# Layer norm variances by four 32-column products over moving squares, own token kept by a mask

## The chip, the cores and the metric

The kernel runs on one core of one Trainium2 chip. A core has five engines that run side by side and meet only through semaphores: TensorE (matrix products, here PE, its weight loads PEld), VectorE (DVE), ScalarE (ACT), GpSimd (POOL) and SyncE (SP, which issues transfers). The metric is the time of one execution on the device in microseconds; shorter is better.

## The reference

Sixteen layers follow each other on an activation `x` of 4 batches, 512 tokens and 128 features. Each adds to `x` what an attention, an expert or feed-forward stage, a state space stage or a recurrent cell makes of the normalised `x`:

```python
def _layernorm(x, axis=-1, eps=1e-05):
    m = jnp.mean(x, axis=axis, keepdims=True)
    v = jnp.var(x, axis=axis, keepdims=True)
    return (x - m) / jnp.sqrt(v + eps)

x = x + _L0_attn_a_ref(_layernorm(x, axis=-1), ...)
x = x + _L0_ffn_ref(_layernorm(x, axis=-1), ...)
... # fourteen more of the same kind
```

So there are 16 x 4 = 64 norms of one batch, 512 tokens by 128 features each. The change touches only how their variances are found and spread.

## The kernel before

**Layout.** `x` and its normalised copy `xn` stay on chip as 128 partitions (the features) by 4 x 512 columns (the tokens of the four batches). A layer works through the batches one after the other; each engine has its own program, written out by hand as a loop over steps, and waits on semaphores where it needs another's result. All constants and weights are loaded by SyncE at the start (`build_program`, L4198; four groups after layer 2), the constants (`const`) right behind `x`, and the first product waits for both.

**One norm of one batch.** Features lie along partitions, so sums over features are products:
- `centre` (L245): TensorE multiplies by (identity minus 1/128), which leaves x minus its mean in a PSUM bank, 128 x 512.
- `square` (L252): ScalarE squares the bank into on-chip memory; `keep` (L259, or L266 on ScalarE) copies the centred values.
- `var` (L273): for each of the TT = 4 tiles of 128 tokens, a product with the tile's squares as the weights (128 x 128) and one column of 1/128 as the moving side. The result is one column: the variance of token p of tile t stands in partition p, column t of the same bank. A float32 product is two weight loads and two matmuls in the records.
- `eps` (L281): VectorE adds 1e-5 to those 128 x 4 numbers, into `small`.
- `rstd` (L287): GpSimd raises them to the power -1/2.
- `diag` (L294): VectorE multiplies the identity, repeated four times, by them: four diagonal 128 x 128 matrices side by side, 128 x 512.
- `spread` (L302): TensorE multiplies by ones, so that every partition has all tokens' factors, 128 x 512.
- `scale` (L310): VectorE multiplies the kept values by it, into `xn`.

**Where it stands.** `NextNorm` (L192) gives these steps to a layer: while a layer works on a later batch, it normalises the finished ones for the next layer, and its steps are put by hand into the layer's loops. The norm of the last batch (`last=True`, names with `in_`) is mostly done at the start of the next layer. Layer 0 has nothing before it, so `normalise` (L113) does its four norms alone, with the same steps at L136 (centre), L142 (variance), L149 (spread), L156, L164, L168, L173 and L180. The order on each engine is fixed by the program: `eps` and `diag` stand in VectorE's queue between the layer's own operations, `rstd` in GpSimd's.

**Layers by kind.** First attention (lines 317 to 594), expert stages (595 to 984, four of the layers), keep (985 to 1653), linear (1654 to 2067), bit (2068 to 2174, two), landmark (2175 to 2826), pairs (2827 to 3051), cell (3052 to 3221, two), state space (3222 to 3777, two), elu (3778 to 4155). In the expert stages L680, L681 and L701 are the experts' products, L687 a product that spreads gates, L747 and L757 VectorE's steps between them. L1228 (keep), L3867, L3871 and L3855 (elu) and L1882 (linear) are products and a VectorE step of those layers; L3527 is the scan of the state space layers.

Of the kernel before, what the change touches and what calls it, by code (L numbers as in the profile page):

```python
# [15 lines left out]
ALU = mybir.AluOpType  # L16
ACT = mybir.ActivationFunctionType
AX = mybir.AxisListType

B, S, D = 4, 512, 128  # L20
P = 128
TT = S // P
LN_EPS = 1e-5
NEG = -1e30
# [86 lines left out]


def normalise(nc, core, name):  # L113
    L = Layer(nc, name, core, [],
              centred=B,
              square=B,
              kept=B,
              var=B,
              eps=B,
              rstd=B,  # L120
# [3 lines left out]
    with L.ctx:  # L124
        centred, square = L.sb("centred", [P, B, S]), L.sb("square", [P, B, S])
        small = L.sb("small", [P, 2, B, TT])
        diag = L.sb("diag", [P, B, TT, P])
        banks = L.ps("banks", [P, B, S])
        ps_var = L.ps("ps_var", [P, B, S])
        eye = core.w("const", "eye")  # L130
        with nc.Block() as block:
            @block.tensor
            def _(pe):
                for step in range(B + 3):
# [4 lines left out]
                    if 0 <= b < B:  # L139
                        pe.wait_ge(L["square"].sem, L["square"].at(0, b + 1))  # L140
                        for t in range(TT):
                            mm = pe.matmul(ps_var[:, b, t:t + 1], square[:, b, t * P:(t + 1) * P],  # L142
                                           core.w("const", "mean", 0, 1), start=True, stop=True)
                        mm.then_inc(L["var"].sem, 1)
# [14 lines left out]
            def _(dve):  # L159
                for step in range(B + 3):  # L160
# [5 lines left out]
                    if 0 <= b < B:  # L166
                        dve.wait_ge(L["var"].sem, L["var"].at(0, b + 1))
                        dve.tensor_scalar(small[:, 0, b, :], ps_var[:, b, 0:TT], LN_EPS, None, ALU.add)\  # L168
                            .then_inc(L["eps"].sem, 1)
                    b = step - 2  # L170
                    if 0 <= b < B:
                        dve.wait_ge(L["rstd"].sem, L["rstd"].at(0, b + 1))
                        dve.tensor_tensor(diag[:, b, :, :], eye.unsqueeze(1).to_broadcast([P, TT, P]),  # L173
                                          small[:, 1, b, :].unsqueeze(2).to_broadcast([P, TT, P]), ALU.mult)\
                            .then_inc(L["diag"].sem, 1)
                    b = step - 3
# [15 lines left out]
class NextNorm:  # L192


    NAMES = ("centred", "square", "kept", "var", "eps", "rstd", "diag", "spread", "xn")
    SIGNALS = {f"nx_{n}": B for n in NAMES}
    LAST = {f"in_{n}": 1 for n in NAMES}

    def __init__(self, L, *banks, steps=1, last=False, shared=None, buffers=None, elsewhere=None, wide=False):
        self.L, self.banks, self.steps, self.last = L, banks, steps, last  # L200
        key = "in" if last else "nx"
        self.first = B - 1 if last else 0
        self.elsewhere = elsewhere or {}
        self.sets = len(banks) if wide else 1
        if buffers:
            self.kept, self.square_sb, self.diag_sb = buffers
            self.small = L.sb(key + "_small", [P, 2, TT])
        elif shared:
            self.kept, self.square_sb, self.small, self.diag_sb = shared.kept, shared.square_sb, shared.small, shared.diag_sb
        else:  # L210
            self.kept = L.sb(key + "_kept", [P, len(banks), S])
            n = self.sets
            self.squares, self.smalls = L.sb(key + "_square", [P, n, S]), L.sb(key + "_small", [P, n, 2, TT])
            self.diags = L.sb(key + "_diag", [P, n, TT, P])
            self.square_sb, self.small, self.diag_sb = self.squares[:, 0, :], self.smalls[:, 0, :, :], self.diags[:, 0, :, :]
        self.centred, self.squared, self.copied, self.var_in, self.eps_in, self.powered, self.diag_in, self.spread_in, \
            self.xn = (L[f"{key}_{n}"] for n in self.NAMES)

# [49 lines left out]
    def var(self, pe, b):  # L268
# [3 lines left out]
        for t in range(TT):  # L272
            mm = pe.matmul(self.bank(b)[:, t:t + 1], self.square_of(n)[:, t * P:(t + 1) * P],  # L273
                           self.L.core.w("const", "mean", 0, 1), start=True, stop=True, skip_group_check=True)
        mm.then_inc(self.var_in.sem, 1)

    def eps(self, dve, b):
        n = b - self.first
        dve.wait_ge(self.var_in.sem, self.var_in.at(0, n + 1))
        dve.wait_ge(self.powered.sem, self.powered.at(0, self.reused(n)))  # L280
        dve.tensor_scalar(self.small_of(n)[:, 0, :], self.bank(b)[:, 0:TT], LN_EPS, None, ALU.add).then_inc(self.eps_in.sem, 1)  # L281

# [7 lines left out]
    def diag(self, dve, b):  # L290
        n = b - self.first
        dve.wait_ge(self.powered.sem, self.powered.at(0, n + 1))
        dve.wait_ge(self.spread_in.sem, self.spread_in.at(0, self.reused(n)))
        dve.tensor_tensor(self.diag_of(n)[:, :, :], self.L.core.w("const", "eye").unsqueeze(1).to_broadcast([P, TT, P]),  # L294
                          self.small_of(n)[:, 1, :].unsqueeze(2).to_broadcast([P, TT, P]), ALU.mult)\
            .then_inc(self.diag_in.sem, 1)

# [3956 lines left out]
def constants():  # L4254
# [10 lines left out]
        "centre": eye - np.float32(1 / D),  # L4265
        "mean": np.full((P, P), 1 / D, np.float32),
        "eye": eye,
# [165 lines left out]
```

## Time and profile before

| | |
|---|---|
| median of 3 runs | 2679.58 us |
| lowest and highest | 2677.96 and 2688.18 us |
| profiled execution, first to last instruction | 2684.0 us |
| TensorE busy | 2287.6 us, 85% |
| VectorE busy | 1742.8 us, 65% |
| ScalarE busy | 1209.6 us, 45% |
| GpSimd busy | 612.0 us, 23% |
| mean granted clock of TensorE | 0.923 |

The profile is of one execution. Busy time is the union of an engine's instructions; a matmul's record is longer than the time after which the next can start, so start-to-start times say more than durations. The granted clock is a share of 2.4 GHz; the other level is 1.2 GHz. In the views, `128*128` is the part of the array that a product takes (rows by columns), `xN` the number of records, and what stands in brackets is the engine's idle time before the instruction and what ended it.

### The profile page before, as it was taken

To read this page: it belongs to the slowest core of one execution; us is meant where nothing else is said; L and a number is where in the kernel's file an instruction comes from. 1 tells how busy PE (TensorE), PEld (TensorE's weight loads), DVE (VectorE), ACT (ScalarE), POOL (GpSimd) and SP (SyncE) were. 2 spreads that over 40 slices of the span, in tenths; PEclk is the share of its full clock that TensorE was granted. 3 is DMA by queue.
4 is the path that set the end of the run, shared out by engine and by line. 5 is a ranking of instruction groups with operands and counts; after the bars stand their busy time and mean duration, and the time that the engine had idled before them with its cause. 6 is when DMAs were issued, how large, how long until landed. Compare 5 with 4: busy or idle time off the path is not lost. (4 is left out here: it accounts for less than half of the span.)

```text
span 2684.0 us, 29577 instructions
## 1 busy us (share of the span) xinstructions
PE 2287.6 (85%) x9624; PEld 994.5 (37%) x9664; DVE 1742.8 (65%) x2454; ACT 1209.6 (45%) x2392; POOL 612.0 (23%) x606
## 2 busy tenths in 40 slices
PE   8999999957569989887999789977879988978877
PEld 3333334412112224354454334423334436533333
DVE  4666665567877735553463754489995446579995
ACT  3555563157647842221342244265544422256542
POOL 1111110042211110021101010056651023046651
PEclk9999999968879979997867889989999999989999
DMA  3000000032000011000000000022110000012110
GB/s 153 1 1 1 1 1 0 0 48 39 10 2 1 1 43 52 1 1 1 0 1 0 0 1 0 1 80 71 64 39 0 1 0 2 1 64 71 63 55 16
DMA packets 19254, 59.67 MB, mean 22 GB/s; under 512 B 2272, under 2 KB 8480, under 8 KB 18208
## 3 DMA queue, kind: packets, MB, share of 16 engines
q1 hardware_dynamic: 18240, 57.01, 6.8%
q10 hardware_dynamic: 864, 0.79, 0.2%
q8 instruction: 79, 1.29, 0.2%
q14 instruction: 71, 0.58, 0.1%
HBM read 50.12 MB, written 1.31 MB: 19 GB/s over the span
## 5 line engine op out<-in xcount | busy, mean ns | idle before, releaser
L3761 POOL TENSOR_TENSOR l_drive<-l_du,l_bsb 128x1024 f32<-128x1024 f32 x126 | 299.8, 2389 | 142.0 <-DVE l_state L3527 113.0
L3527 DVE TENSOR_TENSOR_SCAN l_state<-l_decay,l_drive 128x1024 f32<-128x1024 f32 x128 | 292.8, 2289 | 13.4 <-ACT l_decay L3468 2.1
L3357 PE MATMUL l_py<-l_read,w_const 128*128 128x512 f32 x512 | 261.6, 636 | 0.0
L287 POOL TENSOR_TENSOR l_nx_small<-l_nx_small,w_const 128x4 f32<-128x4 f32 x50 | 53.7, 1075 | 891.6 <-DVE l_nx_small L281 891.6
L3468 ACT ACTIVATE l_decay<-l_delta,l_a 128x511 f32<-128x511 f32 x256 | 165.7, 681 | 169.1 <-DVE l_state L3527 168.9
L426 ACT ACTIVATE l_probs<-l_psp,l_stats 128x512 f32<-128x512 f32 x256 | 173.1, 683 | 150.4 <-DVE l_stats L436 150.4
L1301 DVE TENSOR_REDUCE l_tops<-l_ring 128x2 f32<-128x1024 f32 x128 | 151.5, 1220 | 45.1 <-PE l_ring L1292 44.7
L434 DVE TENSOR_REDUCE l_stats<-l_psp 128x2 f32<-128x1024 f32 x128 | 156.2, 1221 | 35.6 <-PE l_psp L388 35.0
L742 DVE SCALAR_TENSOR_TENSOR l_product<-l_psu,w_gated,l_first 128x512 f32<-128x512 f32 x104 | 78.1, 751 | 134.5 <-ACT l_first L716 134.2
L1373 ACT ACTIVATE l_shared<-l_ring 128x512 f32<-128x512 f32 x256 | 138.9, 598 | 48.9 <-PE l_ring L1363 48.7
L3537 DVE TENSOR_TENSOR l_read<-l_state,l_pc 128x1024 f32<-128x1024 f32 x128 | 153.3, 1198 | 2.9 <-DVE l_state L3527 1.6
L3341 PE MATMUL l_pc<-l_parts,l_spread 96*128 96x512 bf16 x128 | 52.5, 410 | 107.0 <-DVE l_read L3537 106.9
L716 ACT ACTIVATE l_first<-l_psg,w_gated 128x512 f32<-128x512 f32 x104 | 71.4, 687 | 150.9 <-PE l_psu L681 150.9
L3357 PEld LDWEIGHTS l_py<-l_read,w_const 128*128 128x128 f32 x512 | 105.4, 206 | 90.1 <-issue 85.4
L1187 ACT ACTIVATE l_shared<-l_ring,l_mins 128x512 f32<-128x512 f32 (+3 forms) x256 | 121.1, 541 | 39.0 <-PE l_acc L1228 20.2
L388 PE MATMUL l_psp<-l_q,l_k 64*128 64x512 f32 x512 | 127.6, 616 | 1.1 <-ACT l_probs L426 1.1
L757 DVE TENSOR_TENSOR l_held<-l_held,l_psc 128x512 f32<-128x512 f32 x152 | 103.7, 682 | 37.8 <-PE l_psc L687 30.4
L400 PE MATMUL l_ps_ctx<-l_probs,l_vs 128*64 128x512 f32 x512 | 124.2, 605 | 0.5 <-POOL l_vs L475 0.5
L475 POOL TENSOR_TENSOR l_vs<-l_v,l_stats 128x128 f32<-128x128 f32 x128 | 51.3, 401 | 313.8 <-DVE l_stats L442 313.8
L1172 DVE TENSOR_REDUCE l_mins<-l_ring 128x2 f32<-128x1024 f32 (+2 forms) x96 | 99.4, 1039 | 30.9 <-PE l_ring L1155 29.8
L680 PE MATMUL l_psg<-xn,w_gated 128*128 128x512 f32 x208 | 108.1, 602 | 3.3 <-DVE l_product L742 2.6
L681 PE MATMUL l_psu<-xn,w_gated 128*128 128x512 f32 x208 | 106.4, 593 | 0.0
(608 smaller groups left out, 4330.5 us busy)
## 6 DMA issues: line engine op xcount, KB each, us to landing
l_bsb<-l_rows SPq DMA_DIRECT2D x64, 512.0 KB, 3.6
l_stack<-l_parts SPq DMA_DIRECT2D x84, 64.0 KB
w_gated<-in_gated SPq DMA_DIRECT2D x1, 3297.5 KB, 12.4
w_mha<-in_mha SPq DMA_DIRECT2D x1, 2568.5 KB, 13.2
w_ssm<-in_ssm SPq DMA_DIRECT2D x2, 1171.0 KB, 16.4
w_moe<-in_moe SPq DMA_DIRECT2D x1, 2248.0 KB, 18.1
w_const<-in_const SPq DMA_DIRECT2D x1, 1325.0 KB, 7.5
x<-x_in SPq DMA_DIRECT2D x1, 1024.0 KB, 4.7
```

The lines of the kernel that those rows point to most:

```text
L388: mm = pe.matmul(psp[:, u, i, :], k[r, g % 2, kt * P:(kt + 1) * P], q[r, g % 2, :], start=True, stop=True)
L400: mm = pe.matmul(ps_ctx[i * HD:(i + 1) * HD, :], vs[:, s % 4, i, :], probs[:, s % 4, i, :], start=half == 0 and u == 0, stop=half == 1 and ...
L426: act.activation(probs[:, s % 4, i, :], psp[:, s % 2, i, :], ACT.Exp, bias=stats[:, s % 4, 1, i:i + 1], scale=scale, accum_out=stats[:, s ...
L434: dve.tensor_reduce(stats[:, s % 4, 0, :], psp[:, s % 2, :, :], AX.X, ALU.max).then_inc(L["top"].sem, 1)
L1187: act.activation(probs1[qt][:, g, :], ring[:, at + i, lo:lo + N], ACT.Exp, bias=mins[:, s, n:n + 1], scale=-1.0, **kept).then_inc(L["exp1" ...
L1301: dve.tensor_reduce(tops[:, n % 2, t, :], ring[:, 2 * (x % 2):2 * (x % 2) + 2, :], AX.X, ALU.min)\
L1373: act.activation(probs2[:, p % 3, 2 * (x % 2) + i, :], ring[:, 4 + i, :], ACT.Exp, scale=-1.0)\
L3357: mm = pe.matmul(py[:, t, :], eye, read[:, k % 2, t, :], start=False, stop=k % NS == NS - 1, skip_group_check=True)
L3468: act.activation(decay[:, k % 2, t, 1:], delta[:, b % 2, t, 1:], ACT.Exp, scale=a[:, t, n:n + 1])\
L3527: dve.tensor_tensor_scan(state[:, k % 2, :, :].rearrange("p t s -> p (t s)"), decay[:, k % 2, :, :].rearrange("p t s -> p (t s)"), drive[: ...
L3537: dve.tensor_tensor(read[:, k % 2, :, :], state[:, k % 2, :, :], pc[:, :].unsqueeze(1).to_broadcast([P, CT, S]), ALU.mult).then_inc(L["rea ...
L3761: pool.tensor_tensor(drive[:, k % RING, :, :], du[:, :, :], bsb[:, k // 2 % RING, k % 2, :].unsqueeze(1).to_broadcast([P, CT, S]), ALU.mult)\
```

## The change

The squares become the moving side and the weights a 128 x 32 block of 1/128. For tile t the product goes to array columns 32t to 32t+31 and thereby to partitions 32t to 32t+31 of the bank, 128 columns wide: every one of those 32 partitions has the variance of all 128 tokens of the tile. One token of each four-token set belongs to a partition: partition 32t + m keeps the tokens m, 32 + m, 64 + m and 96 + m of tile t. VectorE adds epsilon and multiplies by a 0/1 mask (`own`, four identities of 32 side by side, in all four quarters) in one operation, 128 x 128, and sums each 32 columns in a second, 128 x 4; it waits for its own first result in between. `small` then has 128 x 4 numbers as before, in another order. `diag` multiplies a constant mask of 128 x 512 (`own_token`) by them, so that again each column has one non-zero entry; power, spread and scale are as they were. The constants lose 96 columns of `mean` and gain 128 of `own` and 512 of `own_token`, 544 more columns of 128 float32. Each norm has one more semaphore.

```diff
@@ normalise @@
                         for t in range(TT):
-                            mm = pe.matmul(ps_var[:, b, t:t + 1], square[:, b, t * P:(t + 1) * P],
-                                           core.w("const", "mean", 0, 1), start=True, stop=True)
+                            mm = pe.matmul(ps_var[t * QUAD:(t + 1) * QUAD, b, 0:P], core.w("const", "mean"),
+                                           square[:, b, t * P:(t + 1) * P], start=True, stop=True,
+                                           tile_position=(0, t * QUAD))
...
-                        dve.tensor_scalar(small[:, 0, b, :], ps_var[:, b, 0:TT], LN_EPS, None, ALU.add)\
+                        dve.scalar_tensor_tensor(own[:, b, :], ps_var[:, b, 0:P], LN_EPS, core.w("const", "own"), ALU.add,
+                                                 ALU.mult).then_inc(L["own"].sem, 1)
+                        dve.wait_ge(L["own"].sem, L["own"].at(0, b + 1))
+                        dve.tensor_reduce(small[:, 0, b, :], own[:, b, :].rearrange("p (j c) -> p j c", j=TT), AX.X, ALU.add)\
                             .then_inc(L["eps"].sem, 1)
...
-                        dve.tensor_tensor(diag[:, b, :, :], eye.unsqueeze(1).to_broadcast([P, TT, P]),
-                                          small[:, 1, b, :].unsqueeze(2).to_broadcast([P, TT, P]), ALU.mult)\
-                            .then_inc(L["diag"].sem, 1)
+                        dve.tensor_tensor(diag[:, b, :, :].rearrange("p t (j c) -> p t j c", j=TT), own_tokens(core),
+                                          by_token(small[:, 1, b, :]), ALU.mult).then_inc(L["diag"].sem, 1)
@@ class NextNorm: var, eps, diag @@
         for t in range(TT):
-            mm = pe.matmul(self.bank(b)[:, t:t + 1], self.square_of(n)[:, t * P:(t + 1) * P],
-                           self.L.core.w("const", "mean", 0, 1), start=True, stop=True, skip_group_check=True)
+            mm = pe.matmul(self.bank(b)[t * QUAD:(t + 1) * QUAD, 0:P], self.L.core.w("const", "mean"),
+                           self.square_of(n)[:, t * P:(t + 1) * P], start=True, stop=True, skip_group_check=True,
+                           tile_position=(0, t * QUAD))
         mm.then_inc(self.var_in.sem, 1)
...
-        dve.tensor_scalar(self.small_of(n)[:, 0, :], self.bank(b)[:, 0:TT], LN_EPS, None, ALU.add).then_inc(self.eps_in.sem, 1)
+        own = self.own[:, n % self.sets, :]
+        dve.scalar_tensor_tensor(own, self.bank(b)[:, 0:P], LN_EPS, self.L.core.w("const", "own"), ALU.add, ALU.mult)\
+            .then_inc(self.own_in.sem, 1)
+        dve.wait_ge(self.own_in.sem, self.own_in.at(0, n + 1))
+        dve.tensor_reduce(self.small_of(n)[:, 0, :], own.rearrange("p (j c) -> p j c", j=TT), AX.X, ALU.add)\
+            .then_inc(self.eps_in.sem, 1)
...
-        dve.tensor_tensor(self.diag_of(n)[:, :, :], self.L.core.w("const", "eye").unsqueeze(1).to_broadcast([P, TT, P]),
-                          self.small_of(n)[:, 1, :].unsqueeze(2).to_broadcast([P, TT, P]), ALU.mult)\
-            .then_inc(self.diag_in.sem, 1)
+        dve.tensor_tensor(self.diag_of(n)[:, :, :].rearrange("p t (j c) -> p t j c", j=TT), own_tokens(self.L.core),
+                          by_token(self.small_of(n)[:, 1, :]), ALU.mult).then_inc(self.diag_in.sem, 1)
@@ constants @@
-        "mean": np.full((P, P), 1 / D, np.float32),
+        "mean": np.full((P, QUAD), 1 / D, np.float32),
+        "own": np.tile(np.eye(QUAD, dtype=np.float32), (TT, TT)),
+        "own_token": np.kron(np.eye(TT, dtype=np.float32), np.tile(np.eye(QUAD, dtype=np.float32), (1, TT))),
```

`QUAD` is 32. `own_tokens` gives the mask as partition by tile t, group j, column c; `by_token` repeats the four numbers over the tiles and over the 32 columns of a group.

## Rows read from the trace of the kernel before

**Rows 1.** The page's first part, and the cores view: span and granted clock.

```profile
PE 2287.6 (85%) x9624; PEld 994.5 (37%) x9664; DVE 1742.8 (65%) x2454; ACT 1209.6 (45%) x2392; POOL 612.0 (23%) x606
...
core 0: 2684.0 us, clock 0.923
```

**Rows 2.** Stretches; busy us (x) of PE, PEld, DVE, ACT, POOL; clock, DMA, GB/s.

```profile
31.20:414.00 382.80, 375.18 (x1316) 121.56 (x1316) 252.35 (x492) 220.78 (x579) 54.19 (x131) 1.00 0.00 1
...
1567.80:1739.10 171.30, 167.30 (x469) 76.64 (x476) 83.40 (x139) 72.79 (x117) 9.12 (x8) 0.99 0.00 1
...
2361.70:2646.90 285.20, 219.51 (x512) 89.69 (x512) 262.50 (x185) 149.50 (x222) 164.29 (x74) 0.93 0.18 60
```

**Rows 3.** Timeline of TensorE in a bit stage: start us, busy us, line, form.

```profile
1262.65 1.02 PE L2092 MATMUL l_out<-l_h,w_bitffn 128*128 128x512 f32 x2
1263.51 0.95 PE L273 MATMUL l_first<-w_const,l_in_square 128*128 128x1 f32 x8
1264.32 1.10 PE L2084 MATMUL l_up<-xn,w_bitffn 128*128 128x512 f32 x2
```

**Rows 4.** Timeline of TensorE in keep: four products of 32 columns.

```profile
596.14 0.43 PE L1228 MATMUL l_acc<-l_shared,l_unit 128*32 128x128 f32 x8
596.50 0.39 PE L1150 MATMUL l_ring<-l_stack 64*128 64x512 bf16 x2
```

**Rows 5.** Timeline of TensorE where the form changes, in keep and in elu.

```profile
610.77 1.12 PE L1063 MATMUL l_aux<-xn,w_keep 128*128 128x512 f32 x2
...
2222.65 0.94 PE L3867 MATMUL l_mix<-l_feats,l_state 128*128 128x128 f32 x6
2223.51 1.08 PE L3871 MATMUL l_mix<-l_energy,l_vaug 128*32 128x128 f32 x32
```

**Rows 6.** Timeline of VectorE: three dependent 128x128 steps of an expert stage.

```profile
1591.26 0.27 DVE L801 TENSOR_REDUCE l_small<-l_tie 128x16 f32<-128x128 f32 x1
1591.57 0.29 DVE L803 TENSOR_TENSOR l_chosen<-l_tie,l_small 128x128 f32<-128x128 f32 x1
1591.90 0.29 DVE L807 SCALAR_TENSOR_TENSOR l_key<-l_chosen,l_key 128x128 f32<-128x128 f32 x1
```

**Rows 7.** The first stretch, all weight loads running; GB/s is last.

```profile
0.00:9.40 9.40, 0.00 (x0) 0.00 (x0) 0.00 (x0) 0.08 (x1) 0.19 (x4) 1.00 0.82 326
```

**Rows 8.** Timeline of TensorE in layer 0's own norm.

```profile
13.06 1.71 PE L142 MATMUL n_ps_var<-w_const,n_square 128*128 128x1 f32 x8
14.63 2.05 PE L136 MATMUL n_banks<-x,w_const 128*128 128x512 f32 x2
16.47 1.71 PE L142 MATMUL n_ps_var<-w_const,n_square 128*128 128x1 f32 x8
```

**Rows 9.** Timeline of the linear stage, VectorE and TensorE.

```profile
1192.85 0.69 DVE L1882 TENSOR_TENSOR l_gated<-l_mix,l_u 128x512 f32<-128x512 f32 x1 [5.70 <-ACT l_square L1819]
1193.46 0.15 DVE L281 TENSOR_SCALAR l_nx_small<-l_last 128x4 f32<-128x4 f32 x1
1193.53 0.68 DVE L1873 TENSOR_TENSOR l_state<-l_front,w_const 128x512 f32<-128x512 f32 x1
...
1195.48 0.70 PE L302 MATMUL l_last<-l_nx_diag,w_const 128*128 128x512 f32 x1 [2.34 <-DVE l_nx_diag L294]
```

**Rows 10.** Timeline of an expert stage behind L281.

```profile
493.95 0.68 DVE L757 TENSOR_TENSOR l_held<-l_held,l_psc 128x512 f32<-128x512 f32 x1
...
494.81 0.19 PEld L701 LDWEIGHTS l_out<-l_held,w_moe 128*128 128x128 f32 x1 [0.24 <-DVE l_held L757]
495.24 1.02 PE L701 MATMUL l_out<-l_held,w_moe 128*128 128x512 f32 x2
```

**Rows 11.** Timeline of the elu stage, VectorE and TensorE.

```profile
2263.03 0.16 DVE L281 TENSOR_SCALAR l_nx_small<-l_last 128x4 f32<-128x4 f32 x1 [1.67 <-PE l_last L273]
...
2265.09 1.13 PE L302 MATMUL l_last<-l_nx_diag,w_const 128*128 128x512 f32 x2 [0.41 <-DVE l_nx_diag L294]
```

**Rows 12.** Timeline of a state space stage: what follows L281 (1971.11, 0.15) on VectorE.

```profile
1971.33 2.29 DVE L3527 TENSOR_TENSOR_SCAN l_state<-l_decay,l_drive 128x1024 f32<-128x1024 f32 x1
```

More of the change, by code:

```diff
@@ L22 @@
 TT = S // P
+QUAD = P // TT
 LN_EPS = 1e-5
@@ L104, in batch, with own_tokens, by_token @@
         return self.x[:, bass.ds(b * S, S)]
+def own_tokens(core):
+    return core.w("const", "own_token").rearrange("p (t j c) -> p t j c", t=TT, j=TT)
+def by_token(rstd):
+    return rstd.unsqueeze(1).unsqueeze(3).to_broadcast([P, TT, TT, QUAD])
 def normalise(nc, core, name):
@@ L118, in normalise @@
               var=B,
+              own=B,
               eps=B,
@@ L126, in normalise @@
         small = L.sb("small", [P, 2, B, TT])
+        own = L.sb("own", [P, B, P])
         diag = L.sb("diag", [P, B, TT, P])
@@ L129, in normalise @@
         ps_var = L.ps("ps_var", [P, B, S])
-        eye = core.w("const", "eye")
         with nc.Block() as block:
@@ L192 @@
 class NextNorm:
-    NAMES = ("centred", "square", "kept", "var", "eps", "rstd", "diag", "spread", "xn")
+    NAMES = ("centred", "square", "kept", "var", "own", "eps", "rstd", "diag", "spread", "xn")
     SIGNALS = {f"nx_{n}": B for n in NAMES}
@@ L206, in __init__ @@
             self.kept, self.square_sb, self.diag_sb = buffers
-            self.small = L.sb(key + "_small", [P, 2, TT])
+            self.small, self.own = L.sb(key + "_small", [P, 2, TT]), L.sb(key + "_own", [P, 1, P])
         elif shared:
             self.kept, self.square_sb, self.small, self.diag_sb = shared.kept, shared.square_sb, shared.small, shared.diag_sb
+            self.own = shared.own
         else:
@@ L214, in __init__ @@
             self.diags = L.sb(key + "_diag", [P, n, TT, P])
+            self.own = L.sb(key + "_own", [P, n, P])
             self.square_sb, self.small, self.diag_sb = self.squares[:, 0, :], self.smalls[:, 0, :, :], self.diags[:, 0, :, :]
-        self.centred, self.squared, self.copied, self.var_in, self.eps_in, self.powered, self.diag_in, self.spread_in, \
+        self.centred, self.squared, self.copied, self.var_in, self.own_in, self.eps_in, self.powered, self.diag_in, self.spread_in, \
             self.xn = (L[f"{key}_{n}"] for n in self.NAMES)
```

## The prediction, made before the changed kernel had run

> **What bounds the kernel now.** I read the page's engine line and the cores view first: one core, 2684.0 us, TensorE busy for 85% of it, mean granted clock 0.923 [rows 1]. Then the stretches view, cut by layer: in the first attention and the expert stages TensorE is busy for 98% and VectorE for 66 and 49%; the two bit stages, not shown, are of that kind with 95%. In the state space stages it is VectorE with 92% [rows 2]. So a norm's work on TensorE counts in one kind of stage and its work on VectorE in the other. In the rest (landmark, linear, pairs, keep, elu) I went to the timeline around each variance step (L273) and asked two things: does the VectorE step behind it (L281) wait for the products or stand in VectorE's queue, and does TensorE wait for the end of the chain (L302)?
>
> **The products, old.** In a bit stage at 2.4 GHz the eight records of L273 (a float32 product is two) run from 1263.51 to the next line's start at 1264.32: 0.81 us for eight one-column outputs, set by eight weight loads at 0.10 apiece. The pair that follows is busy 1.10 us where the pair before was 1.02, so 0.08 of its load shows too: 0.89 us in all [rows 3]. The first load is hidden behind the product before.
>
> **The products, new.** L1228 has the new form exactly: four products of 32 weight columns over 128 float32 columns into four partition quarters of one bank. Its eight records take 0.36 us to the next start [rows 4]. To that come the two ends, where the array goes from 128*128 to 128*32 and back and the load isn't hidden: six records of L3867 last 0.86 us before L3871 starts, where 0.11 each would be 0.66 and one exposed first load 0.10, so some 0.10 goes to the change of form; the pair after L1228 is busy 1.12 us against 1.02, 0.10 more [rows 3, 5]. New block: 0.10 + 0.36 + 0.10 = 0.56 us, a saving of 0.33. Bounds: 0.14 (each change of form costs twice that) to 0.53 (neither costs anything).
> The Trainium skill, page "TensorEngine Tiling (Array Packing)", section "Tiling Modes", speaks against this change: switching the tiling mode, not just the tile, drains TensorE. With a drain of a whole 128-column record at each end the block would be near 0.8 us and the forecast some 6 us later, near 2678; the rows just used show changes of form at 0.10 each, so I go by them.
>
> **The variance step on VectorE.** Removed: one 128x4 operation of 0.15 us that overlaps its successor, starting 0.07 before it [rows 9]. Added: a 128x128 scalar_tensor_tensor, a wait of VectorE for its own result, and a 128x128 reduction. The same shapes: reduction 0.27, scalar_tensor_tensor 0.29, and from the start of the first of such a dependent pair to the start of the next 0.31 to 0.33 us [rows 6]. So 0.33 + 0.20 (the reduction, less the overlap with what follows) in place of 0.07 to 0.08: **0.44 us more** on VectorE's queue and on the chain to GpSimd's power. Bounds 0.40 to 0.60. What is queued behind it on VectorE waits; so does GpSimd's L287. The product with the mask (L294) keeps its 128x512 output; its mask is now read in full instead of repeated, and I take nothing for it (bounds -0.05 to +0.1).
>
> **The sum, norm by norm (64 of them).**
> (1) Constants grow by 544 columns, 272 KB; the load stage moves 326 GB/s, and TensorE's first product waits for it [rows 7]: +0.9 us (0 to 1.5).
> (2) The stand-alone norm of layer 0, four batches. TensorE runs at 1.2 GHz there (L142 takes 1.57 us, the pair L136 1.84, and a batch 3.41) [rows 8]. I double the new block: 1.1 in place of 1.57, four times, less 0.44 for the last chain: -1.4 us. VectorE's own work per batch, three steps of 0.68 and the two new ones, 2.6 us, bounds the gain at about -3.
> (3) TensorE-bound blocks: 3 in the first attention, 16 in the expert stages, 6 in the bit stages, 2 in the landmark stage, 1 in a cell: 28 x 0.33 = -9.2 us. Cover: VectorE's 0.44 lies in its idle time, 34 to 51% of these stages [rows 2]. It shows at six blocks of the expert stages where L757 stands right behind L281: L757 ends at 494.63, the load of L701 starts at 494.81, its product at 495.24, and a load needs 0.11, so the slack is 0.32; 6 x 0.12 = +0.7 [rows 10].
> (4) Chains on which both engines wait in turn and L281 waits for the products, as at 2263.03 (1.67 idle, then TensorE 0.41 at L302) [rows 11]: three such chains follow a product of 32 columns, where no change of form is paid on the way in and the first load isn't exposed twice: I estimate 1.0 us falling to 0.3, less 0.44, so 3 x -0.3. Seven more lie at 1.2 GHz, where the products take 1.57 and more [rows 8] and by the doubled block some 0.9 less with the wait for the load, less 0.44: 7 x -0.5. Together -4.4.
> (5) Chains on which L281 is already late because VectorE is at something else: in the linear stage L1882 is at work from 1192.85, L281 follows at 1193.46, and TensorE then idles 2.34 us for L302 [rows 9]. Faster products gain nothing there and the 0.44 is exposed: 3 in the linear stage, 2 in the pairs, 1 each in keep, landmark, elu: 8 x 0.44 = +3.5.
> (6) State space stages: VectorE goes from L281 straight into the scan [rows 12]; four of the eight norms there have no slack: +1.8.
> Sum: 0.9 - 1.4 - 9.2 + 0.7 - 4.4 + 3.5 + 1.8 = **-8.1 us**. The profiled run's span was 2684.0, so its like would be 2675.9; that run lies 4.4 above the median of 2679.6 and inside the three runs (2678.0 to 2688.2). From the median: **2671.5 us**. A difference below 0.5% (13.4 us) is about what a measurement of this kernel can't tell from none, and this forecast lies inside it.
>
> **The rivals.**
> B, the clock comes back sooner. With a mean of 0.923, 15% of the span, some 410 us, is at 1.2 GHz [rows 1]. The one-column products give the array next to nothing to do: in the start stage TensorE is busy end to end from 9.5 to 28.8 us and its pairs still take 1.84 [rows 8]. The new ones stream 128 columns and are followed sooner by real work. If a tenth of the 410 us went back to 2.4 GHz, with TensorE setting half of it, that is 410 x 0.1 x 0.5 x 0.5 = 10 us more: **2661**. Against: most slow stretches come from waits for scans, maxima and L294, which stay.
> C, the slower side: VectorE's two dependent operations, at their upper bound of 0.60 us and with no slack behind L281 anywhere. Then 64 x 0.60 = 38.4 and 0.9 for the constants stand against the products' 9.2, 1.8 and 8.8 (terms 3, 2 and 4 without VectorE's part): +19.5, **2699**; at 0.44 it would be +9.3, 2689. It decides where the slack behind L281 is under the difference of 0.60 and 0.33. Against: VectorE idles 34 to 51% of the stages in question, and the slack found is 0.32.
> D, the change doesn't do what it says: the four products don't overlap. Then eight passes of 0.107 and the ends make 1.16 us in place of 0.89: 28 x 0.27 = 7.6, and with nothing gained in (2) and (4) 5.6, 0.9, 0.7, 3.5 and 1.8 for the rest: +20, **2700**. Against: L1228's 0.36 for the same form [rows 4].
> E, the 0.33 is given back: TensorE comes sooner to a wait for VectorE or ScalarE and stands there. Without term (3): **2680.5**. For: the first attention has all engines in lockstep. Against: almost no idle is shown before TensorE's products there.
>
> **How the numbers follow.** The forecast has 0.49, with its own range of 2664 to 2677 (the bounds of the block alone give -5.6 and +5.3 on 28 blocks); B 0.24, E 0.13, C 0.09, D 0.05. Faster by over 0.5% (under 2666.2): B's 0.23 and 0.10 of the forecast, 0.33. Slower by over 0.5% (over 2693): 0.06 of C and D's 0.05, 0.11. Within: the rest, 0.56. Leaving out C and D and 6 in 100 at the ends, the range is 2658 to 2684.
>
> **What would show each step.** In the profile after: L273's eight records 0.36 us to the next start, and the 128x128 form on 128*32; the pair behind them at 1.12; the two VectorE steps at 0.29 and 0.27 with 0.03 between; the expert stages 1.1 to 1.4 us shorter each, the bit stages 1.0, the linear stage 1.3 longer, the state space stages 0.9 longer; the first product 0.9 later. The forecast is wrong if the mean clock moves by more than 0.003, if the expert stages don't shorten, or if the products start one after another.

## The result, and the profile after

The changed kernel took 2661.1 us (median of 4 runs, 2659.5 to 2665.8) against 2682.5 for the kernel before on the same chip (4 runs, 2678.0 to 2688.2): a ratio of 0.9933, 95% interval 0.9909 to 0.9956. Measured once more, beside two of the experiments, it gave 2663.3 (6 runs, 2656.6 to 2668.7) against 2681.0, ratio 0.9932 [0.9908, 0.9956]. So it is some 18 us faster by the ratio, 0.67% (21 by the medians): more than the 13.4 us that I had called indistinguishable, though the low end of the interval, 0.44%, isn't. It is inside the range, 10 us below the forecast, and a gain of more than twice the forecast 8.1.

The page and the cores view of the kernel after, to be held against [rows 1]:

```profile
PE 2251.3 (85%) x9624; PEld 933.3 (35%) x9664; DVE 1758.9 (66%) x2518; ACT 1209.4 (45%) x2392; POOL 611.5 (23%) x606
...
core 0: 2664.0 us, clock 0.923
```

TensorE has 36 us less work and 61 us less of weight loads in the same number of instructions, VectorE 16 us more in 64 more. The mean clock is that of before. The span went from 2684.0 to 2664.0, 20.0 less. Where it came from is read stage by stage, each from the first instruction of its lines to the first of the next stage's; "at 1.2" is the time in the stage for which the trace's record of the granted clock shows 1.2 GHz (it has nothing for the start stage):

| stage | before, us (at 1.2) | after, us (at 1.2) | difference | forecast |
|---|---|---|---|---|
| start, with layer 0's own norm | 31.2 | 25.9 | -5.4 | -0.5 |
| first attention | 382.8 (0) | 381.5 (1) | -1.3 | -1.0 |
| four expert stages | 586.8 (11) | 579.5 (7) | -7.4 | -4.6 |
| two bit stages | 84.1 (6) | 81.0 (5) | -3.0 | -2.0 |
| linear | 133.7 (42) | 136.3 (46) | +2.6 | +1.3 |
| landmark | 144.9 (89) | 146.5 (86) | +1.6 | -0.2 |
| pairs | 80.5 (34) | 83.5 (41) | +3.0 | +0.9 |
| keep, elu, two cells | 667.6 (153) | 668.0 (157) | +0.5 | -3.9 |
| two state space stages | 572.2 (79) | 561.7 (68) | -10.5 | +1.8 |

(The seven 1.2 GHz chains of term (4), -3.5, which the forecast didn't place by stage, are all put into the row of keep, elu and the cells.) Seven of the nine rows missed the forecast by more than 1 us, and in opposite directions. The stretches that answer to [rows 2], and the start:

```profile
25.90:407.40 381.50, 373.88 (x1317) 118.95 (x1317) 253.50 (x495) 220.67 (x579) 54.09 (x132) 1.00 0.01 2
1562.60:1730.60 168.00, 163.83 (x469) 72.51 (x475) 85.11 (x144) 72.79 (x117) 9.12 (x8) 1.00 0.00 1
2347.30:2626.70 279.40, 214.64 (x512) 84.55 (x512) 259.29 (x190) 149.44 (x222) 164.35 (x74) 0.95 0.19 61
0.00:25.90 25.90, 11.96 (x49) 3.67 (x49) 9.59 (x20) 3.67 (x5) 5.36 (x8) 1.00 0.93 383
```

In the state space stage VectorE (the third busy figure) has less to do than before, 259.3 against 262.5 us, with five more operations. That is the surprise of this case: something on VectorE got cheaper that the change wasn't about.

The new block on TensorE, in a bit stage, timeline as in [rows 3]:

```profile
1266.42 1.02 PE L2114 MATMUL l_out<-l_h,w_bitffn 128*128 128x512 f32 x2
1267.37 0.43 PE L290 MATMUL l_aux<-l_nx_square,w_const 128*32 128x128 f32 x8
1267.73 1.13 PE L2106 MATMUL l_up<-xn,w_bitffn 128*128 128x512 f32 x2
```

From L290's first start to the next line's 0.36 us, where L273 had 0.81; the pair behind it 1.13, so 0.11 for the change of form on the way out; and on the way in 0.95 from L2114's first start to L290's, 0.09 more than the 0.86 after which L273 began [rows 3]. Together 0.56, as built up from L1228. (By the Trainium skill's "TensorEngine Tiling (Array Packing)", section "Tiling Modes", the array drains at a change of mode; what these rows show of it is 0.1 us each way.)

One caution for all that follows. Stages whose code is untouched differ between executions with the clock. The keep stage of the old form lasted 464.6, 460.1, 458.2 and 457.8 us in four profiles, with 136, 106, 106 and 109 us of it at 1.2 GHz. With the new form it lasted 464.5 us in the changed kernel, and in six further profiles of this study 454.6 to 463.5. The kernel before ran from 2667.0 to 2693.0 in the course of this study. So below I compare stages, and totals only as medians.

### The profile page after: what moved, and what is told of

Same layout as the page of the kernel before. It is cut to its first block and busy times, and to the rows that moved or that the text cites. A ratio compares the mean times of both kernels' runs of the same rounds, so it can differ in the third digit from the quotient of the medians.

```text
span 2664.0 us, 29641 instructions
## 1 busy us (share of the span) xinstructions
PE 2251.3 (85%) x9624; PEld 933.3 (35%) x9664; DVE 1758.9 (66%) x2518; ACT 1209.4 (45%) x2392; POOL 611.5 (23%) x606
## 5 line engine op out<-in xcount | busy, mean ns | idle before, releaser
L3783 POOL TENSOR_TENSOR l_drive<-l_du,l_bsb 128x1024 f32<-128x1024 f32 x126 | 299.8, 2389 | 136.3 <-DVE l_state L3549 108.4
L723 PE MATMUL l_out<-l_held,w_gated 128*128 128x512 f32 x208 | 106.1, 593 | 0.3 <-issue 0.3
```

The costliest lines, as they stand in the source:

```text
L3783: pool.tensor_tensor(drive[:, k % RING, :, :], du[:, :, :], bsb[:, k // 2 % RING, k % 2, :].unsqueeze(1).to_broadcast([P, CT, S]), ALU.mult)\
```

## The experiments

**The start stage: what brought 5.4 us?** Two kernels. The first has the new form in `normalise` alone, the other 60 norms as before (larger constants kept). The second has no new form at all (larger constants kept here too), but in `normalise` the old products stream 128 columns each, and VectorE's 128x4 step reads every 128th column of what they write:

```diff
-  mm = pe.matmul(ps_var[:, b, t:t + 1], square[:, b, t * P:(t + 1) * P],
-                 core.w("const", "mean", 0, 1), start=True, stop=True)
+  mm = pe.matmul(ps_var[:, b, t * P:(t + 1) * P], square[:, b, t * P:(t + 1) * P],
+                 core.w("const", "mean", 0, 1).to_broadcast([P, P]), start=True, stop=True)
```

> The new form in the stand-alone norm of layer 0 alone; the other 60 norms keep the old products, the 128x4 step and the identity as mask. The larger constants stay. My forecast's step (2): the start stage 0.5 us shorter (-1.4, +0.9 for the constants), its pairs still at 1.84 us. Clock theory: the new products give the array columns to stream, so the clock is at 2.4 GHz again from about 14.5 us on, pairs at 1.0 to 1.1 us, start stage 25.9 us in place of 31.2 (-5.4), and the total about 5 below the kernel before. If the rest of the start stage's gain came from somewhere else than the norm, the stage stays above 29.

> All norms old. In the stand-alone norm of layer 0 alone the old products, squares as weights and as many weight loads as before, stream 128 equal columns each instead of one; the variance step then reads every 128th column. No product is shorter, no VectorE operation is added, results are the same. If the clock answers to the columns that go through the array: 2.4 GHz comes back as early as in the new form, the start stage shortens by 3 to 5 us although each block has more to do. If only the shorter block matters (less work at 1.2 GHz, an earlier end of the stage): the stage gets 0 to 2 us longer, at 1.2 GHz to its end.

Measured: new form alone, start stage 25.4 us, every layer but keep and the expert stage before it within 0.2 of before; total 2674.8 us, ratio 0.9994 [0.9979, 1.0010]. Old form with 128 columns, start stage 26.4 us, total 2672.7, ratio 0.9979 [0.9963, 0.9996]. The timeline of TensorE in the second kernel (columns as in [rows 3]), to be held against [rows 8]:

```profile
13.80 1.92 PE L154 MATMUL n_ps_var<-w_const,n_square 128*128 128x128 f32 x8
15.51 1.23 PE L148 MATMUL n_banks<-x,w_const 128*128 128x512 f32 x2
16.58 1.05 PE L154 MATMUL n_ps_var<-w_const,n_square 128*128 128x128 f32 x8
17.47 1.02 PE L148 MATMUL n_banks<-x,w_const 128*128 128x512 f32 x2
```

The first block is longer than the old one (1.71 to the next start, against 1.57), as more columns go through at the 1.2 GHz level. But the pair behind it takes 1.23 and the next 1.02, where the kernel before had 2.05 [rows 8]; there it stayed at that level for all but the last record of the stage:

```profile
24.87 4.82 PE L149 MATMUL n_banks<-n_diag,w_const 128*128 128x512 f32 x6
```

The six records start 0.99, 0.85, 0.85, 0.85 and 0.68 us apart, and the last, at 29.10, is 0.59 us long. The stretches view shows a clock of 1.00 for all of this, and can't be used: the trace's record of the granted clock has no entry before its first one at 2.4 GHz. That entry stands at 28.8 us in the kernel before and at 28.7 and 30.0 in the two other profiles with one-column blocks in this stage; in the ten profiles with 128 columns per product, new form or old, it stands at 13.5 to 15.9. The number of weight loads is the same and VectorE has no added operation. The blocks of the two kernels differ in nothing but the columns that the products stream: with one column each TensorE was busy by the record, and the clock stayed at 1.2 GHz; with 128 each it came up 13 us sooner, though each block had more to do. At 13.5 us, in the first kernel, the rise even came 0.27 us ahead of its first new block, so the first two pairs alone can be enough; in the kernel before they were not, and it did not come between the one-column blocks that followed. It was rival B's mechanism, shown at the one place where it had been sitting in plain view: in [rows 8] TensorE is busy from end to end and slow. The changed kernel has it too:

```profile
14.10 0.53 PE L154 MATMUL n_ps_var<-n_square,w_const 128*32 128x128 f32 x8
14.56 1.12 PE L148 MATMUL n_banks<-x,w_const 128*128 128x512 f32 x2
```

The total of the first kernel moved by less than its start stage (3.1 us by the medians, with an interval that contains both 0 and 5.4), so what the 5.4 is worth in the total is known only to some 3 us.

**The state space stages: what brought 10.5 us?** By-form groups of the product with the mask whose output is `l_square`, before and after (line engine op, out<-in, form, count; then busy us and mean ns):

```profile
L294 DVE TENSOR_TENSOR l_square<-w_const,l_nx_small 128x512 f32<-128x512 f32 x8 | 17.6, 2200 | 2.2 <-POOL l_nx_small L287 2.2
```

```profile
L317 DVE TENSOR_TENSOR l_square<-w_const,l_nx_small 128x512 f32<-128x512 f32 x8 | 9.0, 1125 | 2.2 <-POOL l_nx_small L310 2.2
```

8.6 us of the 10.5 are there, and they come from four of the eight. Two more, the first of each stage, take 2.35 us in both kernels: at 1746.08 before, 0.08 us behind the start of a GpSimd cast (L3743, 1.89 us), and at 1737.49 after, just as far behind the same cast. The change left those as they were. One of the four in the timeline of VectorE and GpSimd, before and after:

```profile
1974.63 2.34 POOL L3761 TENSOR_TENSOR l_drive<-l_du,l_bsb 128x1024 f32<-128x1024 f32 x1
1974.64 2.88 DVE L294 TENSOR_TENSOR l_square<-w_const,l_nx_small 128x512 f32<-128x512 f32 x1
```

```profile
1966.27 0.73 DVE L317 TENSOR_TENSOR l_square<-w_const,l_nx_small 128x512 f32<-128x512 f32 x1
1966.41 2.80 POOL L3783 TENSOR_TENSOR l_drive<-l_du,l_bsb 128x1024 f32<-128x1024 f32 x1
```

Before, GpSimd's product started 12 ns ahead of VectorE's, and VectorE's took 2.88 us; after, VectorE's starts 140 ns ahead, takes 0.73, and GpSimd's takes 2.80 in place of 2.34. VectorE's product is 2.19 us longer than its 0.69 elsewhere when GpSimd's 2.34 are ahead of it, and GpSimd's is 0.46 longer when 0.59 of VectorE's are left at its start. One waits for nearly all of the other. The Trainium skill, page "SBUF — State Buffer", section "Who interferes with whom", says this: the two engines share a pair of ports under an exclusive lock, and the order of issue decides who blocks. The rows agree; both products read two tiles of on-chip memory that is not PSUM.

Why did the order change? GpSimd's power starts 0.08 us after the variance step ends, in all of these kernels; VectorE's scan, where it follows the step directly, starts 0.20 to 0.22 us after the step's start, whether the step is short or long. Behind the 128x4 step of 0.155 us the scan is 19 ns ahead of the power (1971.33 [rows 12] and 1971.35); behind the reduction of 0.286 it is 163 ns ahead:

```profile
1962.76 0.29 DVE L303 TENSOR_REDUCE l_nx_small<-l_nx_own 128x4 f32<-128x128 f32 x1
1962.96 2.28 DVE L3549 TENSOR_TENSOR_SCAN l_state<-l_decay,l_drive 128x1024 f32<-128x1024 f32 x1
1963.12 1.01 POOL L310 TENSOR_TENSOR l_nx_small<-l_nx_small,w_const 128x4 f32<-128x4 f32 x1 [6.28 <-DVE l_nx_small L303]
```

So it is GpSimd that the longer step holds back, not VectorE that comes sooner. (What holds the scan for 0.215 us behind the short step, where L1873 follows L281 after 0.07 [rows 9], isn't shown.)

Three edits shift one engine against the other. In the kernel before, in these two stages:

```diff
-  dve.tensor_scalar(small[:, 0, :], bank[:, 0:TT], LN_EPS, None, ALU.add)
+  dve.tensor_scalar(wide[:, :], bank[:, 0:P], LN_EPS, None, ALU.add)   # GpSimd reads wide[:, 0:TT]
```

> The kernel before, with one edit in the two state space stages: the 128x4 step L281 works on 128x128 (GpSimd's power reads its first four columns). The old products, the old mask, the identity, stay. The step costs VectorE 0.1 to 0.15 us more. Phase theory (the 128x4 step is so short that the scan behind it starts late and GpSimd's product then stands 10 ns ahead of VectorE's product with the mask; a longer step puts VectorE ahead): that product falls from 2.88 to 0.73 us at four places, each state space stage 3.5 to 5 us shorter, total 7 to 10 us below the kernel before. Rival, the gain comes from the new mask operand or the shorter products: the product with the mask stays at 2.88, the stages get 0.3 us longer.

And in the changed kernel, behind L303 in these two stages (first with 128x4, then with 128x256):

```diff
+  dve.tensor_scalar(idle[:, :], core.w("const", "minus_half", 0, TT), LN_EPS, None, ALU.add)
```

> The changed kernel, with one edit in the two state space stages: behind the reduction L303 stands one more VectorE operation of 128x4 that nobody reads, so that the scan starts behind a short operation again while GpSimd's power starts at the reduction's end as now. Phase theory: the product with the mask takes 2.7 to 2.9 us again at the four places where it now takes 0.73, and the two stages grow by 8 to 10 us together, to 2670 in all. Rival (the new mask operand or the products made it short): it stays at 0.73 and the stages grow by the operation itself, 8 x 0.2 = 1.6 us.

> The changed kernel with a 128x256 VectorE operation of about 0.42 us, which nobody reads, behind the reduction in the two state space stages. The 128x4 operation put there before moved the scan by only 0.06 us and left VectorE's product with the mask 74 ns ahead of GpSimd's. This one moves VectorE by 0.33 us or more while GpSimd's power starts as before, so GpSimd's product must come first. Phase theory: the product with the mask takes 2.7 to 2.9 us again at four places, the two stages together 8 to 12 us longer than in the changed kernel, total about 2670. Rival (what made it short is the new mask operand or the new products): it stays at 0.73, the stages grow by the operation itself, at most 8 x 0.33 = 2.6 us.

Measured, at the first of the four places in each kernel (the other three agree within 0.02 us), with the two kernels of the next experiment:

| kernel | products | step | mask | VectorE's start ahead of GpSimd's, ns | product with mask, us | two stages against before, us |
|---|---|---|---|---|---|---|
| before | old | 128x4 | old | -12 | 2.88 | 0 |
| products alone | new | 128x4 | old | -14 | 2.88 | +0.5 |
| after, 128x256 behind | new | new | new | -64 | 2.83 | +3.9 |
| after, 128x4 behind | new | new | new | +74 | 0.68 | -10.4 |
| step 128x128 | old | 128x128 | old | +131 | 0.72 | -12.8 |
| steps alone | old | new | old | +140 | 0.73 | -9.8 |
| after | new | new | new | +140 | 0.73 | -10.5 |

The sign of the one column sets the other, whatever products and mask. The kernel before with nothing but the wider step took 2668.8 us, ratio 0.9966 [0.9949, 0.9983]: half the gain of the whole change for an edit that only makes an operation longer; its scan still starts 0.215 us after the step's start, the power 0.13 later than before. The 128x256 one took the gain of these stages away again, 2671.2 in all, ratio 0.9970 [0.9955, 0.9984]: they are 14.4 us longer than in the changed kernel, more than the 8 to 12 expected, with 21 us more at 1.2 GHz. With 128x4 behind I was wrong: I had thought that it would bring the collision back, and the lead only fell from 140 to 74 ns (2658.4 us in all, ratio 0.9923 [0.9906, 0.9939]); the scan was moved by 0.07 us only. The row of the long one shows it at the place:

```profile
1959.65 2.34 POOL L3787 TENSOR_TENSOR l_drive<-l_du,l_bsb 128x1024 f32<-128x1024 f32 x1
1959.71 2.83 DVE L321 TENSOR_TENSOR l_square<-w_const,l_nx_small 128x512 f32<-128x512 f32 x1
```

**The change in halves.** One kernel has the new products and the old 128x4 step and mask; the other has the old products and the new pair of steps, fed with the four old columns (`(j c)` is short for the view by four groups of 32):

```diff
+  dve.scalar_tensor_tensor(own (j c), bank[:, 0:TT].unsqueeze(2).to_broadcast([P, TT, QUAD]), LN_EPS,
+                           core.w("const", "own") (j c), ALU.add, ALU.mult)
```

> The new products alone: the variance step is the old 128x4 one on the first four columns of what they write, the mask is the identity. So each token is divided by the wrong token's deviation, numbers change, the work doesn't. My term (3): 0.33 us less at each TensorE-bound block, the stages of the first attention 1.0, the expert stages 1.3 and the bit stages 1.0 shorter each. Terms (4) and (5): without VectorE's 0.44 nothing gets longer: linear 0, pairs 0, landmark -0.7, elu -0.9 or more. Clock theory for linear and pairs (the new products leave the array less busy or stand at other times, so that 2.4 GHz comes later): these get longer by 1 to 3 us even without the VectorE part. State space stages by the phase theory: the 128x4 step is back, the collision with it, so no gain, within 1 us.

> The two new VectorE operations alone in the 60 norms of the layers, behind the old products (the four old columns, each repeated 32 times, are multiplied by the mask and summed: the same shapes, the same result). My term (5): 0.44 us at each exposed chain, linear 1.3, pairs 0.9 longer, keep, landmark and elu 0.4 each. Cover of term (3): the first attention and the bit stages 0, the expert stages 0 to 0.3 longer each, since VectorE idles there. Rival C (the dependent steps are on the path everywhere): the first attention, the expert and the bit stages 0.4 us longer for each of their 25 norms, 10 us in all. State space stages by the phase theory: the reduction in front of the scan alone takes the collision away, 9 to 13 us shorter in the two together, with the old products and the old mask.

Measured: products alone, where each token is divided by another token's deviation, 2655.6 us (4 runs), ratio 0.9914 [0.9882, 0.9946]; steps alone 2690.8 (8 runs), ratio 1.0042 [1.0018, 1.0067]. By stage against before, us, with the change in time at 1.2 GHz in brackets:

| stage | products alone | steps alone | both |
|---|---|---|---|
| first attention | +0.2 (+4) | 0.0 (0) | -1.3 (0) |
| four expert stages | -5.4 (+0) | +2.0 (+4) | -7.4 (-4) |
| two bit stages | -2.6 (+1) | +0.1 (-2) | -3.0 (-1) |
| linear | +0.1 (+2) | +1.9 (+4) | +2.6 (+4) |
| landmark | -0.7 (0) | +6.5 (+11) | +1.6 (-2) |
| pairs | +1.3 (+4) | +0.6 (+1) | +3.0 (+7) |
| elu | -3.8 (0) | +2.4 (+10) | +0.5 (+4) |
| keep | -3.2 (-7) | +8.2 (+15) | -0.1 (-1) |
| two cells | -4.4 (-4) | +3.2 (+5) | +0.1 (+1) |
| two state space stages | +0.5 (+3) | -9.8 (-10) | -10.5 (-10) |

Several of these miss what was expected: the first attention gained nothing with the products alone (1.0 expected; 4 us more at 1.2 GHz), and with the steps alone landmark and elu grew by far more than the 0.4 each. The linear stage is the cleanest. TensorE's product with the spread deviations waits for VectorE's mask product 2.34 us before [rows 9]; with the products alone, the steps alone, and both:

```profile
1183.43 1.22 PE L319 MATMUL l_last<-l_nx_diag,w_const 128*128 128x512 f32 x1 [3.10 <-DVE l_nx_diag L311]
```

```profile
1206.46 0.70 PE L323 MATMUL l_last<-l_nx_diag,w_const 128*128 128x512 f32 x1 [2.79 <-DVE l_nx_diag L315]
```

```profile
1186.31 1.22 PE L324 MATMUL l_last<-l_nx_diag,w_const 128*128 128x512 f32 x1 [3.56 <-DVE l_nx_diag L317]
```

The products add 0.76 to the wait, which is what TensorE saves ahead of it, net nothing; the steps add 0.45, a net loss, three times 0.45 = 1.35 us. VectorE, behind L1882 before and L1904 after, is why:

```profile
1183.23 0.69 DVE L1904 TENSOR_TENSOR l_gated<-l_mix,l_u 128x512 f32<-128x512 f32 x1 [5.70 <-ACT l_square L1841]
1183.83 0.28 DVE L300 SCALAR_TENSOR_TENSOR l_nx_own<-l_last,w_const 128x128 f32<-128x128 f32 x1
1184.15 0.29 DVE L303 TENSOR_REDUCE l_nx_small<-l_nx_own 128x4 f32<-128x128 f32 x1
1184.35 0.68 DVE L1895 TENSOR_TENSOR l_state<-l_front,w_const 128x512 f32<-128x512 f32 x1
```

From L300's start to the next operation 0.52 us, against 0.07 for L281 [rows 9]: 0.45 more. The remaining 1.2 us of the linear stage's 2.6 go with the clock: behind the first of the three waits L324 now takes 1.22 us and not 0.70, and 4 us more of the stage are at 1.2 GHz.

**The cover in the TensorE-bound stages.** In the changed kernel, ahead of L300 in the first attention, the expert and the bit stages:

```diff
+  dve.tensor_scalar(idle[:, :], core.w("const", "ones_s", 0, 2 * P), LN_EPS, None, ALU.add)
```

> The changed kernel with one more VectorE operation of 128x256 (about 0.4 us, read by nobody) ahead of the two variance steps in the first attention, the expert and the bit stages, 28 norms. It doubles what the change adds on VectorE there. My reading of the cover: it is hidden except at the six blocks of the expert stages where the next product's operand stands right behind it, at most 6 x 0.4 = 2.5 us in all. Rival C: 0.4 us at each, 11 us.

Measured: 2658.1 us (5 runs, 2650.9 to 2665.2), ratio 0.9920 [0.9892, 0.9948], no longer than the changed kernel. The seven stages took 1045.0 us against 1042.0 and, in its second profile, 1042.4 without it; 2 us more of them were at 1.2 GHz, which at a TensorE-bound place is 1 us, so some 2 us are the operation's. It turned out to last 0.29 and not 0.4 us, so it is less than a doubling, and it stands in 27 norms, not 28; 27 x 0.29 = 7.8 us would have shown, and 3 at most did. With the steps alone, above, the same stages grew by 2.1 us, with 3 us more at 1.2 GHz. VectorE's added work is covered there but for 1 to 2 us, and rival C falls.

**A kernel of both forms.** First the changed kernel with the old form back in the linear, landmark, pairs and elu stages; then that with the old form also in the state space stages, with the 128x128 step. The changed kernel ran beside them.

```diff
+  self.form = "old" if L.name in ("l4", "l6", "l8", "l12") else "new"      # second kernel: and "l10", "l14"
```

> The changed kernel once more, unchanged, beside the kernel before and the next two, for an interval narrow enough to judge the 0.5%. If the first measurement holds: 17 to 22 us below the kernel before, ratio 0.992 to 0.9935. If part of its gain was the luck of one chip: under 13 us.

> The changed kernel, but with the old products, the old variance step and the identity in the linear, landmark, pairs and elu stages. My term (5), as far as it goes for these stages (7 x 0.44 = 3.1 us, less term (4)'s gain there of 0.9 at the elu chains): 2 us below the changed kernel. By its profile (linear +2.6, landmark +1.6, pairs +3.0, elu +0.5 against before): these stages go back to 133.7, 144.9, 80.5 and 119.7 us and the total falls by 7.7 us, to about 2653. If those stages differ by when the clock falls and rises in a run rather than by the norms: no difference in the medians.

> As the kernel with the old form in the linear, landmark, pairs and elu stages, and in the two state space stages too, there with the 128x4 step widened to 128x128 as tried alone before. The new form is left in the stand-alone norm, the first attention, the expert, bit, keep and cell stages. If the gains of single stages add: start -5.4, first attention -1.3, expert -7.4, bit -3.0, state space -12.8 (in place of -10.5 with the new form), sum -30 against the kernel before, near 2650, and 8 to 10 us below the changed kernel. If the other stages drift by the clock and eat it: above 2656.

Measured: the changed kernel 2663.3; old form in the four stages 2660.4 (2659.4 to 2666.9), ratio 0.9928 [0.9904, 0.9951]; both forms 2655.5 (2654.6 to 2659.9), ratio 0.9908 [0.9884, 0.9933]. The last is the lowest median of a kernel that does all of the work, 8 us below the changed kernel, but the intervals overlap: it is likely, not shown, to be the faster. Nor did the stages add up as I had it. The linear stage came back to 133.9 and 133.6 us, against 136.3 and 138.1 in the two profiles of the changed kernel. But landmark took 147.5 and 147.3 with its old code, 2.5 more than before, with 4 us more at 1.2 GHz (146.5 and 150.3 in the two profiles of the changed kernel), pairs 81.3 in both (83.5 and 81.6 there), elu 123.1 and 119.8, and the state space stages gained 9.6 and not 12.8, though the product with the mask took 0.70 to 0.71 at all four places. The same code in a stage had more or less of its time at 1.2 GHz from kernel to kernel, with nothing changed in the stage itself; that part of a stage's gain or loss doesn't transfer. (That it hangs on when the stage before ended is likely, not shown.)

## Why the prediction was right or wrong

**Right: the price of the block, and of the pair of steps.** 0.56 us was built from L1228 and two changes of form, and is what the rows show; 0.44 on VectorE came out as 0.45 (0.28 and 0.29 long, 0.03 between). L1228 was the same form in the same kernel, which is better than any rule. Rival D, no overlap, falls with the 0.36 of the timeline. (Its price didn't follow from the other terms: eight passes of 0.107 and the two ends of 0.10 are 1.06, not 1.16, and eleven chains at 0.44 are 4.8, not 5.6.)

**Right in kind, small: term (3).** Forecast for the first attention, the expert and the bit stages: 25 x 0.33 less 0.7 = -7.6; measured -11.7. Those stages had 4.5 us less at 1.2 GHz than before, worth half of that, 2.3 us, where TensorE sets the end; so some -9.4 is the blocks', 0.38 each. 25 x 0.33 is 8.3: the block was sized right. Whether the 0.7 for L757's slack was there stays open: with the steps alone these stages grew by 2.1 us, of which the clock explains some 1.5. Rival E, that the gain would be given back, falls.

**Wrong: term (2), the stand-alone norm, -1.4 where about -6 came** (-5.4 with 0.9 of later start, first product at 10.38 against 9.49). I costed the new products at 1.2 GHz because the old ones ran there, and never asked whether the clock would stay there with the new ones. I had written the answer under rival B, "give the array next to nothing to do", and used it for a total and not for this place. The step that failed is "I double the new block".

**Wrong in sign: term (6), the state space stages, +1.8 where -10.5 came.** The step was "L281 straight into the scan, no slack, so 0.44 each". It added the length of an operation to the chain and took every other operation's length as fixed. But L294 there was 2.88 us long where the same shape took 0.69 elsewhere. I had a group of eight with a mean of 2200 ns in the trace of before, next to one of 39 with 688, and didn't ask why. The whole of it hung on 12 ns. I don't think that a forecast could have known to which side the change would tip it; it could have said that 4 x 2.2 us were at stake there.

**Wrong in sign: terms (4) and (5), the chains.** With the three blocks of landmark and cell counted in term (3), the linear, landmark, pairs, keep, elu and cell stages were to gain 1.9 us and lost 7.7. The whole miss, 9.6 us, is the largest after that of term (6). The mechanism of (5) holds, and its size too, 0.45 a norm in the linear stage; in the elu stage's chain TensorE waits 0.89 at L324 against 0.41, as

```profile
2251.43 1.13 PE L324 MATMUL l_last<-l_nx_diag,w_const 128*128 128x512 f32 x2 [0.89 <-DVE l_nx_diag L317]
```

shows beside [rows 11], while the block ahead of it is shorter by more, 2.98 us from L290 to L324 against 3.15 before. What I left out is what goes with a longer wait on TensorE, more time at 1.2 GHz: with the steps alone, the four stages of landmark, elu, pairs and linear grew by 11.4 us, of which 7 x 0.45 = 3.2 are the operations, and had 27 us more at 1.2 GHz, which at half speed is up to 13. With its old code landmark moved by 2.5 and elu by 3.4 too, so how much of the 7.7 belongs to the change, and whether the waits or the stages' times in the run set the clock, stays open; only the linear stage's 2.2 to 4.4 us was seen in all five profiles of it with the new form.

**The rivals.** B had 0.24 and its total, 2661, is the measured one, but by luck: its mechanism gave 5 us in one stage, not 10 through the kernel (the mean clock of the profiled execution is unchanged at 0.923; in the second measurement the six executions had 0.925 on the mean against 0.923 for the eleven of before, so some of the total may be clock). The rest came from the blocks and from the collision of VectorE and GpSimd. The forecast's misses, -4.9 in the start, -4.1 in term (3), +9.6 in the chains and -12.3 in the state space, come to -11.7 together, more than the forecast's own 8.1. The range held because it was wide and because the 9.6 in the chains took back part of the rest. That the total fell inside it owes something to luck: the largest miss was a gain forecast as a loss.

## What to carry to other kernels

Ahead of pricing a change, look for an operation that lasts far longer at one place than the same shape elsewhere, and see what another engine started just ahead of it. Here two engines collided, and an edit that moved one of them by 0.1 us gave or took 2 us at each place. Then try shifting that place alone; here it was worth half of the change. And where TensorE is busy but slow, ask what streams through it, and read its level from the durations: here blocks of eight weight loads for one column each filled the profile's busy time, and the clock came up 13 to 16 us later than with 128 columns each.

## What the runs showed of the hardware that was not expected

- VectorE's product of two operands in on-chip memory outside PSUM and GpSimd's hold each other up for nearly their whole length, and an order of some nanoseconds decides. Over the four places of all kernels here, VectorE's took 2.83 to 2.89 us with GpSimd ahead by 5 to 65 ns, and 0.68 to 0.73 with VectorE ahead by 68 to 145, GpSimd's then 2.79 to 2.82 in place of 2.34. VectorE's scan did not do this: in the kernel before one ran from 1971.33 to 1973.62, and GpSimd's product began at 1972.32 and took 2.35. One of the scan's two operands, `decay` (L3255), is in PSUM.
- At those places GpSimd's power started 0.08 us after the end of the variance step, and VectorE's scan 0.20 to 0.22 us after the step's start, for steps of 0.155 and of 0.28 us alike.
- Streaming 128 equal columns through each product in place of one, at the same number of weight loads, made the start stage 4.8 us shorter, by an earlier rise of the clock.
- Going from 128*128 to 128*32 products and back cost 0.09 and 0.11 us.
